# Splitting the expert's gated activation anew over DVE, ACT and POOL in a two-layer gated cross-attention kernel

## What is computed

```python
h = einsum('th,ehd->etd', xn, w1) + b1[:, None, :]
a = minimum(h[..., ::2], 7.0)
b = clip(h[..., 1::2], -7.0, 7.0)
s = a * sigmoid(1.702 * a) * (b + 1.0)
y = einsum('eti,eih->eth', s, w2) + b2[:, None, :]
t = einsum('eth,te->th', y, gate_full)
```

## Time and profile before

| | |
|---|---|
| median of 3 runs | 617.11 us (614.41 to 617.48) |
| profiled execution: span from its first to its last instruction | 609.8 us |
| mean granted clock of PE over the span | 0.829 of full |
| busy PE / weight loads / DVE / ACT / POOL | 498.0 / 357.7 / 356.5 / 229.1 / 264.5 us |
| expert stage | 306.9 to 541.0 us of the span |

### The profile page before, as it was taken

The page is one execution under the profiler, slowest core; times in us unless marked ns, Lnnn a source line. Parts: engine busy times, 40 slices in busy tenths (PEclk is TensorE's granted clock), DMA queues, the critical chain, the costliest instruction groups (busy, mean ns, idle before and its releaser), DMA issues. The chain is left out here.

```text
span 609.8 us, 8643 instructions
## 1 busy us (share of the span) xinstructions
PE 498.0 (82%) x2977; PEld 357.7 (59%) x2977; DVE 356.5 (58%) x849; ACT 229.1 (38%) x409; POOL 264.5 (43%) x286
## 2 busy tenths in 40 slices
PE   1259997999699959994499999699959998967786
PEld 1248885887588748883355455355535554523545
DVE  0745432543254235442469999969996999584320
ACT  0121221122112311222276665376547655724411
POOL 7999931990199745000034442423342344340000
PEclk9999755975597658775599989799979998977888
DMA  7121102110223121002000000000000000000001
GB/s 216 28 73 50 35 1 85 37 35 1 85 103 104 34 69 34 0 0 69 0 1 0 1 1 1 0 1 2 0 0 0 0 1 1 0 1 0 18 18 34
DMA packets 13440, 17.38 MB, mean 28 GB/s; under 512 B 1840, under 2 KB 9954, under 8 KB 13412
## 3 DMA queue, kind: packets, MB, share of 16 engines
q1 hardware_dynamic: 9804, 12.98, 6.8%
q10 hardware_dynamic: 3032, 1.96, 1.2%
q0 software_dynamic: 576, 2.10, 1.1%
HBM read 15.98 MB, written 1.05 MB: 28 GB/s over the span
## 5 line engine op out<-in xcount | busy, mean ns | idle before, releaser
L358 POOL TENSOR_TENSOR rings<-rings 128x512 f32<-128x512 f32 x32 | 42.7, 1335 | 93.6 <-DVE rings L1231 89.3
L768 PE MATMUL bank<-xhl,w_hi 128*128 128x512 f32 (+1 forms) x128 | 78.4, 613 | 1.4 <-ACT rings L510 1.4
L507 ACT ACTIVATE rings<-bank,b1c 128x512 f32<-128x512 f32 x64 | 44.1, 689 | 71.9 <-POOL rings L358 31.4
L429 ACT ACTIVATE wide<-bank 120x512 f32<-120x512 f32 x64 | 36.2, 597 | 83.8 <-PE bank L666 83.8
L358 POOL TENSOR_TENSOR wide<-rings 128x512 f32<-128x512 f32 x32 | 42.1, 1315 | 57.1 <-DVE rings L1231 54.9
L1011 DVE TENSOR_REDUCE nt<-bank 128x4 f32<-128x480 f32 x64 | 39.2, 653 | 46.6 <-PE bank L646 46.6
L646 PE MATMUL bank<-ks,qs 32*128 32x120 f32 x512 | 52.1, 311 | 3.8 <-DVE qs L1003 3.8
L666 PE MATMUL bank<-qs,ks 32*120 32x128 f32 x512 | 53.3, 318 | 1.9 <-DVE qs L1018 1.0
L666 PEld LDWEIGHTS bank<-qs,ks 32*120 32x120 f32 x512 | 49.7, 211 | 6.0 <-DVE qs L1018 5.8
L305 POOL TENSOR_TENSOR bft<-bw,bfly 128x256 f32<-128x256 f32 x34 | 30.0, 882 | 51.7 <-DMA bw<-in_L_ffn_down_weights 27.4
L769 PE MATMUL bank<-xhl,w_lo 128*128 128x512 f32 (+1 forms) x128 | 52.4, 409 | 0.0
(11 more groups left out here) (226 smaller groups left out, 917.2 us busy)
## 6 DMA issues: line engine op xcount, KB each, us to landing
bw<-in_L_ffn_up_weights SPq DMA_DIRECT2D x9, 512.0 KB, 3.7
bw<-in_L_ffn_down_weights SPq DMA_DIRECT2D x9, 512.0 KB, 3.7
bw<-in_L_ffn_w POOLq DMA_DIRECT2D x4, 512.0 KB, 4.3
x_sb<-in_x SPq DMA_DIRECT2D x4, 256.0 KB, 5.1
out<-xr SPq DMA_DIRECT2D x4, 256.0 KB, 2.3
ctx_in<-in_ctx SPq DMA_DIRECT2D x4, 240.0 KB, 2.9
bfly<-in_L_ffn_W_exp ACTq DMA_DIRECT2D x1, 256.0 KB
wcon<-in_L_ffn_W_con ACTq DMA_DIRECT2D x1, 256.0 KB
```

What stands on the lines that cost most here:

```text
L358: pool.tensor_tensor(es[e % len(es)], ea[:, e % 2, :], ec[:, e % 2, :], ALU.mult).then_inc(s["m_s"], 1)
L507: act.activation(ea[:, e % 2, :], SB[1 + e % 2][:, :], ACT.Identity, bias=b1c[:, 0, e:e + 1]).then_inc(s["m_a"], 1)
L768: pe.matmul(bk[:, :], w1_hi[:, e, branch, :], low(g), start=True, stop=False)
```

## The change

For each expert, DVE now reads a's bank, adds the bias and clamps in one instruction, and writes `ea`. ACT evaluates the one function a*sigmoid(1.702a) on `ea`, and evicts b's bank as before; it has two instructions per expert in place of three. DVE clamps `eb` into `ec`, and multiplies `esg` by the gate's bank into `eq`. POOL multiplies `eq` by `ec`. DVE has three instructions per expert in place of four. PE's next use of a's bank waits for DVE's read (`m_a`) in place of ACT's (`m_sg`). The number of DVE's own marks per group falls from 81 to 49.

```diff
--- before.py
+++ after.py
@@ -354,8 +354,9 @@
             def product(g, e):
                 n = g * E + e + 1
                 pool.wait_ge(s["m_ec"], n)
+                pool.wait_ge(s["m_eq"], n)
                 need(pool, "m_y", n - len(es))
-                pool.tensor_tensor(es[e % len(es)], ea[:, e % 2, :], ec[:, e % 2, :], ALU.mult).then_inc(s["m_s"], 1)
+                pool.tensor_tensor(es[e % len(es)], eq[:, e % 2, :], ec[:, e % 2, :], ALU.mult).then_inc(s["m_s"], 1)
 
             def inverse_root(k, n):
 
@@ -502,13 +503,9 @@
             def mixture(g):
                 for e in range(E):
                     n = g * E + e + 1
-                    act.wait_ge(s["m_ha"], n)
-                    need(act, "m_s", n - 2)
-                    act.activation(ea[:, e % 2, :], SB[1 + e % 2][:, :], ACT.Identity,
-                                   bias=b1c[:, 0, e:e + 1]).then_inc(s["m_a"], 1)
+                    act.wait_ge(s["m_a"], n)
                     need(act, "m_eq", n - 2)
-                    act.activation(esg[:, e % 2, :], SB[1 + e % 2][:, :], ACT.Sigmoid, scale=ALPHA,
-                                   bias=b1c[:, 2, e:e + 1]).then_inc(s["m_sg"], 1)
+                    act.activation(esg[:, e % 2, :], ea[:, e % 2, :], ACT.Gelu_apprx_sigmoid).then_inc(s["m_sg"], 1)
                     act.wait_ge(s["m_hb"], n)
                     need(act, "m_ec", n - 2)
                     act.activation(eb[:, e % 2, :], (SB[3], PK)[e % 2][:, :], ACT.Identity,
@@ -763,7 +760,7 @@
             def up(g, e):
 
                 n = g * E + e + 1
-                for branch, bk, read, done in ((0, HA[e % 2], "m_sg", "m_ha"), (1, HB_[e % 2], "m_eb", "m_hb")):
+                for branch, bk, read, done in ((0, HA[e % 2], "m_a", "m_ha"), (1, HB_[e % 2], "m_eb", "m_hb")):
                     need(pe, read, n - 2)
                     pe.matmul(bk[:, :], w1_hi[:, e, branch, :], low(g), start=True, stop=False)
                     pe.matmul(bk[:, :], w1_lo[:, e, branch, :], high(g), start=False, stop=False)
@@ -1217,18 +1214,17 @@
             def mixture(g):
                 for e in range(E):
                     j, n = e % 2, g * E + e + 1
-                    dve.wait_ge(s["m_a"], n)
-                    own.mark(dve.tensor_scalar(ea[:, j, :], ea[:, j, :], LIMIT, None, ALU.min))
+                    dve.wait_ge(s["m_ha"], n)
+                    need(dve, "m_sg", n - 2)
+                    dve.tensor_scalar(ea[:, j, :], SB[1 + j][:, :], b1c[:, 0, e:e + 1], LIMIT, ALU.add, ALU.min
+                                      ).then_inc(s["m_a"], 1)
+                    dve.wait_ge(s["m_eb"], n)
+                    need(dve, "m_s", n - 2)
+                    dve.tensor_scalar(ec[:, j, :], eb[:, j, :], LIMIT + 1.0, 1.0 - LIMIT, ALU.min, ALU.max
+                                      ).then_inc(s["m_ec"], 1)
                     dve.wait_ge(s["m_sg"], n)
                     dve.wait_ge(s["m_gb"], n)
-                    dve.scalar_tensor_tensor(eq[:, j, :], esg[:, j, :], SIG_LIMIT, (PQ, PO)[j][:, :],
-                                             ALU.min, ALU.mult).then_inc(s["m_eq"], 1)
-                    dve.wait_ge(s["m_eb"], n)
-                    own.mark(dve.tensor_scalar(eb[:, j, :], eb[:, j, :], LIMIT + 1.0, 1.0 - LIMIT, ALU.min, ALU.max))
-                    dve.wait_ge(s["m_eq"], n)
-                    own.wait()
-                    need(dve, "m_s", n - 2)
-                    dve.tensor_tensor(ec[:, j, :], eb[:, j, :], eq[:, j, :], ALU.mult).then_inc(s["m_ec"], 1)
+                    dve.tensor_tensor(eq[:, j, :], esg[:, j, :], (PQ, PO)[j][:, :], ALU.mult).then_inc(s["m_eq"], 1)
                     if not first(g):
                         if e == LAG - 1:
                             rows_again(g - 1)
@@ -1264,7 +1260,7 @@
             router_chosen(0)
             router_gates(0)
             mixture(0)
-            OWN_B, PER_B = own.base + own.n, 81
+            OWN_B, PER_B = own.base + own.n, 49
             with dve.Fori(1, G - 1) as g:
                 own.base, own.n = OWN_B + (g - 1) * PER_B, 0
                 mixture(g)
```

## The result

The changed kernel takes 637.22 us (median of 4 runs, 636.95 to 640.94) against 615.76 for the kernel before (4 runs): a ratio of 1.0385, 95% interval 1.033 to 1.0439. It is slower, as forecast, but by 3.9% (21.5 us) where 648 against 617.1 would have been 5.0% (31 us). The profiled execution took 636.95, of which the span is 635.1; forecast were 640.8, and before it was 609.8.

What follows compares the result with a forecast made beforehand. PE and DVE were taken to bound the expert stage by turns. Experts 188.8, blocks 69.5, stretches 2.0, loads 2.8 and PE's clock 2.0 made 265.1 us against 234.1, so 648 against 617.1; range 630 to 663 (8 in 10).

Steps and rivals of the forecast that it cites:

- an expert of 2.95: Loop of one expert on DVE, from a to the next a: 2.95 us, 188.8 for 64.
- a hand-over of 1.32: Between the end of DVE's a and the clamp of `eb`, DVE stands for ACT's two instructions: 1.32 us per expert.
- a clamp at the SBUF rate: Rival: DVE's bank clamp runs 0.27 us faster per expert, 17 us in all, partly eaten by PE: 634; chance 0.09.
- break-even hand-over of 0.84: Hand-over from a's end to the clamp's start at which the stage breaks even, with an expert of 2.47 us.
- a's part: Start of the loop: DVE's bank clamp of a, 0.69 us, plus its signal, 0.03.
- The loads: ACT's table loads at e = 11 delay DVE: 0.3 us in groups 1 and 2, 2.2 in group 3; sum 2.8.
- Stretched clamps: POOL's second task meets DVE's clamp of `eb` in four places, 0.5 us each: 2.0.
- PE's clock: Lower granted clock after PE's stops for `router_top` in groups 1 and 2, 1 us each: 2.0.
- The blocks: Router, residual and norm work behind DVE's last instruction of an expert, not overlapped by ACT: 69.5 us.
- The step from the span to the median: From the profiled execution's 640.8 us to the runs' median, 7.3 above the span before: 648.1.
- What I said of PE: PE waits more, and for DVE; its stops until `router_top` in groups 1 and 2 get longer.
- cold-PE rival: PE gets half clock between blocks, quiet slots grow from 2.95 to 4.44 us; one in four costs 11: 659; chance 0.13.

Runs made afterwards that it cites:

- inside copy: Changed kernel plus a 128 x 128 ACT copy per expert between the function and b's eviction: 651.57 us, ratio 1.0597 to the kernel before.
- outside copy: Changed kernel plus the same ACT copy per expert, placed ahead of ACT's wait for DVE's a: 640.85 us, ratio 1.0386 to the kernel before.
- b first: Changed kernel with ACT's order turned, evicting b before evaluating the function: 596.98 us, ratio 0.9687 to the kernel before.
- next a ahead: Changed kernel with DVE evicting a of expert n + 1 before the clamp and product of n: 603.47 us, ratio 0.9809 to the kernel before.
- bank clamp alone: Kernel before, its SBUF clamp of a replaced by a gate-bank read into a spare tile, a left unclamped: 618.52 us, ratio 1.006.
- clamp behind the function: Changed kernel with ACT's function reading a's bank and the clamp moved into DVE's product: 582.07 us, ratio 0.9439 to the kernel before.

## Why the prediction was right, and what was off

*The mechanism held.* The forecast was an expert of 2.95, a hand-over of 1.32 and 80 us of waits in 64 places; the trace has 2.96, 1.27 and 84.5 in 64. The inside copy showed that ACT's time between DVE's two instructions is paid by the expert, the outside copy that ACT's other time is not, and b first, with ACT's two instructions exchanged, that this order is the cause. With the time alone it could have been luck: 637.22 lies nearer to the rival's 634 (a clamp at the SBUF rate) than to my 648, and only the clamp's 0.744 in the trace rules that rival out. The break-even hand-over of 0.84 was not measured as such; b first, at 2.31 per expert, is on the faster side of it, and it was faster.

*The terms of the loop.* The bank clamp took 0.744, not 0.69, so the upper bound, the product of two tiles, was too low by 0.05: a's part was 0.78 and not 0.72. Function to b's eviction was 0.54 (0.57 forecast; the 0.03 of the SBUF source were named and left out), b's eviction with its signal 0.70 (0.72). These cancel to 0.01. The rival of a clamp at the SBUF rate fell: 0.744 from a bank, 0.436 in SBUF (L1223). The Trainium skill ("VectorE: DVE Perf Modes", section "Why PSUM operands drop a tier") has a PSUM operand held to the single rate in fp32, and the trace agrees.

*The rest of the stage.* 64 x 2.96 = 189.4 (188.8 forecast). The loads: of the 84.5 us of waits 64 x 1.27 = 81.3 are the plain hand-over, so 3.2 are left for them (2.8 forecast). They were where they were put: the wait at e = 11 was 1.50 in group 1, 0.23 more than 1.27 (0.3 forecast), and 3.63 in group 3, 2.36 more (2.2 forecast):

```profile
422.88 0.43 DVE L1223 TENSOR_SCALAR rings<-rings 128x512 f32<-128x512 f32 x1 [1.50 <-ACT rings L511]
```

```profile
557.16 0.43 DVE L1223 TENSOR_SCALAR rings<-rings 128x512 f32<-128x512 f32 x1 [3.63 <-ACT rings L511]
```

The Trainium skill ("ScalarE: Activation LUTs", section "Table sets: the hidden batching unit") would have put 8 us more on them; the load was 1.28 here as before, and began before the wait it precedes was over (307.60, ahead of the function's start at 309.06), so the measurement decides for the trace's figure.

*The terms that were too large.* Stretched clamps: 2.0 forecast; the mean of L1223 is 436 ns against 0.43 undisturbed, and the one that stood out took 0.99, 0.56 more, so some 0.6. PE's clock: 2.0 forecast; DVE waited 0.4 us for PE in the stage after its first instruction, so no more than that. The blocks: 261.1 - 189.4 - 3.2 - 0.6 - 0.4 = 67.5 (69.5 forecast). That figure had been a difference of two totals in which the stretches were estimated from means. Together 5.0 too much; with the others, 4.0: the stage was 261.1, not 265.1.

*Outside the stage.* I had let nothing change there. In the trace it is 1.4 more ahead of it and 3.2 less behind it. The tail's granted clock was 0.87 in place of 0.80. No step of the change touches either stretch, and I did not find out why the clock differs.

*The step from the span to the median* failed, and it was the largest single miss. I added 7.3 us, the distance of the median of before from the profiled execution's span, as time around the span. But each run's own time and span are known now, and they differ by 1.8 to 1.9 in every one (636.95 and 635.1; 613.21 and 611.4). What the section on time and profile before says of the 7.3 us, that they lie around the span, is wrong by the rest. The rest of the 7.3 was that the profiled execution of before was one of the quicker ones: among the runs of before in the two comparisons above the spans went, for example, from 609.5 at a granted clock of 0.826 to 619.2 at 0.815. The changed kernel's profiled execution is within 0.3 of its median. So of the 10.8 us between forecast and result 5.7 are in the span, and the other 5.1 are this. For the same reason the two profiled spans differ by 25.3 us and the medians by only 21.5.

*What I said of PE was half right.* It did wait more in total: 261.1 - 227.2 = 33.9 us not busy against 21.2 of before. But the stop for `router_top` shrank from 12.6 to 5.3. I had argued that longer slots make it longer. My reading of why not: PE is now held at DVE's pace from expert to expert, so it comes to that point later and finds DVE less far behind; it was not tried by itself. The cold-PE rival was rightly not the case: the stage kept 0.92 (0.95 before). The lower clock did come between blocks, such as 0.55 from 335 to 340 us, but cost DVE only the 0.4 us above.

*Where DVE's shorter list went.* DVE is busy in the stage for 33.7 us less (206.8 to 173.1), and not busy for 261.1 - 173.1 = 88.0 in place of 234.1 - 206.8 = 27.3, 60.7 more. 60.7 - 33.7 = 27.0, the stage's loss: the whole gain and 27 us on top were turned into standing at the clamp (84.5, where all waits of before together were 19.0).

## What to carry to other kernels

When a step is moved from one engine to another, write down the round trips inside each in-order queue before the totals: a queue that waits in its own middle for an engine which waits for that queue's beginning paid the other's instructions once per iteration here (1.27 us in 64 places), and the shorter list did not make up for it. Cheapest cure first: exchange the two instructions of the other engine (40 us here), put independent blocks into the gap (41 us, over a third of them because POOL stretched the blocks less), or remove the dependence (55 us, by a clamp behind a monotone stretch of the function). And a wait of 80 us may be free: look whether the engine at its other end waits for a third.

## What the hardware showed that I had not expected

PE can be granted the lower clock while it is busy, for longer than I had thought. In the profiled execution of the outside copy the granted clock was 0.50, all at the 1.2 GHz level, from 303 to 321 us with PE busy for 17.9 of 18 us; in the changed kernel PE had been idle for half of 303 to 308.4 at 0.50, and then, busy throughout, was granted 0.98:

```profile
303.00:321.00 18.00, 17.89 (x37) 10.12 (x37) 8.90 (x17) 7.69 (x15) 5.11 (x4) 0.50 0.00 1
```

```profile
303.00:308.40 5.40, 2.47 (x8) 1.97 (x9) 2.65 (x15) 1.38 (x2) 0.00 (x0) 0.50 0.00 0
308.40:321.00 12.60, 12.60 (x41) 7.15 (x40) 7.50 (x14) 5.32 (x9) 4.53 (x4) 0.98 0.00 1
```

In the first, experts are 309.04 - 305.46 = 3.58 us apart on DVE, not 2.96, and by 330 us the waits for PE have cost 3.3 us more. This contradicts a sentence of the prediction, that a cold PE is then busy without a break "and so warms": it was busy and did not, for 17 us. The profiled executions of the next a ahead (306 to 320 us), the bank clamp alone and the clamp behind the function (310 to 325 us each) show the same, busy throughout at 0.50. What sets the moment at which the clock rises stays open. And POOL's product stretches some of DVE's instructions in SBUF, but not the clamp that reads a bank (0.75 at 308.28 in the changed kernel, with POOL idle, and 0.75 at 310.60 in b first, with POOL beside it): a clamp in SBUF took 1.11 to 1.14 in the first experts of b first, where the trace of before had shown 0.92 and 0.42 without POOL; the small instruction L1106 of the router took 1.31 beside it in the changed kernel and 0.23 without.
